# New order of TensorE's steps in the experts, the cross-attention and the feed-forward of a four-module transformer kernel

## What is computed

```python
# L0: experts. cond and ctx (77 rows) are given per batch
nx = layer_norm(x); k, v = ctx @ Wk, ctx @ Wv
weights = softmax(nx @ Wq @ k.T / 16)                    # 77 keys
combined = concat([nx, weights @ v, cond])
probs = softmax(combined @ router_W + router_b)          # 3 experts
h = silu(combined @ e_w1[e] + e_b1[e])                   # 256*3 -> 512 each
routed = sum(probs[e] * (h @ e_w2[e] + e_b2[e]))
g = sigmoid(silu(combined @ gate_w1) @ gate_w2)
x = x + g * (routed @ out_w + out_b)
# L1: self-attention, cross-attention, feed-forward, 16 heads of 16
x = x + attn(ln(x), ln(x)) + t_sa; x = x + attn(ln(x), ctx, mask) + t_ca
x = x + gelu(ln(x) @ w1 + b1) @ w2 + t_mlp               # 256 -> 1024 -> 256
# L2: the same three with modulated norms and gates, tanh gelu
# L3: cross-attention with adaptive norms of both sides
```

## Time and profile before

| what | us |
| --- | --- |
| median of three runs | 3690.1 (3686.6 to 3706.2) |
| profiled execution | 3701.9 |
| its span, first to last instruction | 3700.1 |
| TensorE busy | 3394.4 |
| ScalarE busy | 2302.2 |
| VectorE busy | 2223.0 |
| GpSimd busy | 871.0 |

### The profile page before, as it was taken

How to read it: one execution, slowest core, us unless ns; L and a number is a source line. 1 busy time by engine, 2 the same in 40 slices (tenths; PEclk the granted TensorE clock), 3 DMA queues, 4 the chain that set the end, 5 groups by cost and what they waited for, 6 DMA issues and landing times.

```text
span 3700.1 us, 60840 instructions
## 1 busy us (share of the span) xinstructions
PE 3394.4 (92%) x22433; PEld 2000.9 (54%) x22433; DVE 2223.0 (60%) x3645; ACT 2302.2 (62%) x3983; POOL 871.0 (24%) x578
## 2 busy tenths in 40 slices
PE   8999998999899898998998889989998899899988
PEld 6767766444643564446444744455446444564465
DVE  2323324794397556953794559746955488549654
ACT  2333332787578555875786457865875578658764
POOL 0322322103400431015103420052024200340061
PEclk8989989999999999999999999999999999999999
DMA  5011012110100001110010010100100101000100
GB/s 184 1 36 35 2 36 63 32 16 26 39 8 14 13 13 57 14 30 31 13 16 15 12 57 11 22 26 26 14 19 13 58 7 26 24 28 11 22 13 13
DMA packets 226988, 101.25 MB, mean 27 GB/s; under 512 B 159951, under 2 KB 210322, under 8 KB 226582
## 3 DMA queue, kind: packets, MB, share of 16 engines
q1 hardware_dynamic: 201734, 77.21, 8.4%
q10 hardware_dynamic: 24976, 20.15, 1.8%
HBM read 79.31 MB, written 9.96 MB: 24 GB/s over the span
## 4 chain that ended last, share of the span: by engine, by line
PE 79%; DVE 12%; ACT 5%; issue 2%; POOL 1%; DMA 0%; SPq 0%; ACTq 0%; DVEq 0%; POOLq 0%
PE ps L736 76%; DVE mxh L1791 4%; PE ps L1184 2%; DVE ctxk L1740 2%; DVE ow L1823 1%; ACT probs L1470 1%; DVE tok L1526 1%; PE ps L1045 1%; DVE small L1510 1%; DVE x L1757 1%; DVE mx L1788 1%; POOL small L1847 1%; ACT qs L1439 1%; ACT whole L1424 1%; ACT hT L1256 1%
## 5 line engine op out<-in xcount | busy, mean ns | idle before, releaser
L1470 ACT ACTIVATE probs<-ps 128x512 f32<-128x512 f32 (+1 forms) x2176 | 1220.4, 639 | 222.3 <-PE ps L736 169.7
L1791 DVE TENSOR_REDUCE mxh<-ps 128x2 f32<-128x1024 f32 x1024 | 1232.1, 1220 | 101.2 <-PE ps L736 96.3
L736 PE MATMUL ps<-probs,v 128*32 128x256 f32 (+2 forms) x8064 | 732.8, 435 | 9.7 <-ACT probs L1470 6.3
L736 PE MATMUL ps<-ks,qs 64*128 64x512 f32 x2048 | 502.4, 491 | 51.5 <-DVE mxh L1791 23.3
L736 PEld LDWEIGHTS ps<-ks,qs 64*128 64x128 f32 x2048 | 193.0, 183 | 445.8 <-issue 347.7
L736 PE MATMUL ps<-qs,ks 64*128 64x512 f32 x2048 | 425.5, 413 | 4.0 <-DVE mxh L1791 3.0
L1911 POOL TENSOR_TENSOR hT<-hT,tok 128x512 f32<-128x512 f32 (+1 forms) x32 | 40.9, 1279 | 1221.1 <-DMA tok<-weights_of_outputs 1221.1
L736 PEld LDWEIGHTS ps<-probs,v 128*32 128x32 f32 (+1 forms) x8064 | 160.0, 107 | 302.7 <-ACT probs L1470 249.1
L736 PEld LDWEIGHTS ps<-qs,ks 64*128 64x128 f32 x2048 | 244.0, 184 | 127.6 <-ACT probs L1470 105.9
L1788 DVE TENSOR_REDUCE mx<-ps 128x4 f32<-128x312 f32 x384 | 166.3, 477 | 150.9 <-PE ps L736 147.4
L736 PE MATMUL ps<-hT,slot 128*128 128x512 f32 x448 | 235.5, 659 | 21.2 <-issue 8.5
(11 more groups left out here) (226 smaller groups left out, 5893.9 us busy)
## 6 DMA issues: line engine op xcount, KB each, us to landing
qs<-mx SPq DMA_DIRECT2D x896, 0.5 KB, 2.0
slot<-in_L_w SPq DMA_DIRECT2D x8, 1024.0 KB, 10.0
slot<-in_L_fc_w SPq DMA_DIRECT2D x8, 1024.0 KB, 5.2
hT<-ow SPq DMA_DIRECT2D x48, 128.0 KB, 2.7
tok<-weights_of_outputs SPq DMA_DIRECT2D x192, 32.0 KB, 1.9
xin<-in_x ACTq DMA_DIRECT2D x5, 1024.0 KB, 5.9
x_after_block<-x ACTq DMA_DIRECT2D x20, 256.0 KB, 2.3
xin<-x_after_block SPq DMA_DIRECT2D x5, 1024.0 KB, 5.5
```

Source lines behind the costliest of these rows:

```text
L736: return pe.matmul(out, lhsT, rhs, start=start, stop=stop)
L1470: ins = act.activation(dst, src, ACT.Exp, scale=SCALE)
L1791: dve.tensor_reduce(mxh[:, z, t, j // 2, j % 2, :], ps[:, a:a + 2, :], AX.X, ALU.max, negate=True).then_inc(dve_done, M.add(dve_done, name))
```

## The change

In the experts, for all but the first pass, the first two key products go ahead of the scores and wait only for what the pass before had done by its gate products. In the first pass they also go ahead of the scores, behind the same waits. VectorE copies them first. Only two first-layer groups stand ahead of the turn of the weights, the other two behind it. `affine_split` writes `hTh` and `whole` of one column block before those of the other. In the cross-attentions `OT` goes behind `PV` and the second pair of `S`. In front of a feed-forward two `up` of half 0 stand ahead of the turn of half 1, and GpSimd's `rsqrt` of half 1 stands at `N` 1, behind its split of half 0, instead of behind `o` 3.

```diff
@@ pass_schedule, cross_attention @@
             if u < len(units):
                 put(tag, ("S",) + units[u] + (0,), *last[4 * u:4 * u + 2])
-            if u > lag:
-                put(tag, ("OT",) + units[u - lag - 1][:2])
             if u >= lag:
                 put(tag, ("PV",) + units[u - lag], ("O",) + units[u - lag][:2])
             if u < len(units):
                 put(tag, ("S",) + units[u] + (2,), *last[4 * u + 2:4 * u + 4])
+            if u > lag:
+                put(tag, ("OT",) + units[u - lag - 1][:2])
...
-        put(follow, ("T", 0), ("N", 1), ("T", 1), *[("up", 0, m) for m in range(FM)])
+        put(follow, ("T", 0), ("N", 1), ("up", 0, 0), ("up", 0, 1), ("T", 1), *[("up", 0, m) for m in range(2, FM)])
@@ tensor, experts @@
+                def last(sem, *steps):
+                    return M.upto("experts", it - 1, sem, steps)
+
+                def evidence_of_keys(e):
+
                     b, act_was, dve_was = take(("L0", "u", e), dve=("L0", "u", e))
-                    pe.wait_ge(act_done, upto(act_done, *act_was))
-                    pe.wait_ge(dve_done, upto(dve_done, *dve_was))
+                    if e < 2 and it:
+                        pe.wait_ge(act_done, last(act_done, ("next", "kv"), *act_was))
+                        pe.wait_ge(dve_done, last(dve_done, *dve_was))
+                    else:
+                        pe.wait_ge(act_done, upto(act_done, *act_was))
+                        pe.wait_ge(dve_done, upto(dve_done, *dve_was))
...
+                if not it:
+                    owner.clear()
+                    pe.wait_ge(act_done, upto(act_done))
+                    pe.wait_ge(dve_done, upto(dve_done))
+                held = [evidence_of_keys(e) for e in range(2)]
+                if it:
+                    owner.clear()
+                    owner.update({b: ("dve", ("L0", "u", e)) for e, b in enumerate(held)})
+                    pe.wait_ge(act_done, upto(act_done))
+                    pe.wait_ge(dve_done, upto(dve_done))
+                for n in range(NH):
...
+                for e in range(2, E + 1):
+                    evidence_of_keys(e)
...
-                early = [hidden(0, m) for m in range(4)]
+                early = [hidden(0, m) for m in range(2)]
...
                     ins.then_inc(mm_done, M.add(mm_done, ("L0", "wT", n)))
+
+                early += [hidden(0, m) for m in range(2, 4)]
@@ scalar, affine_split @@
-                for c in range(KC):
+                    act.wait_ge(mm_done, upto(mm_done, (tag, "T", n, KC - 1)))
                     act.activation(whole[:, KC * n + c, :], ps[:, M.where((tag, "T", n, c)), :], ACT.Identity, bias=shift(c),
@@ vector, experts @@
+                for e in range(2):
+                    keys_copied(e)
                 for n in range(NH):
...
-                for e in range(E + 1):
...
+                for e in range(2, E + 1):
+                    keys_copied(e)
@@ gpsimd, blocks @@
-                    elif kind == "o" and step[1] % 2 and tag in NEXT_LN:
+                    elif kind == "o" and step[1] % 2 and tag in NEXT_LN and not (step[1] == 3 and NEXT_LN[tag] in ("ln2", "ln6")):
                         rsqrt(upto, NEXT_LN[tag], step[1] // 2)
+                    elif kind == "N" and step[1] and KIND[tag] == "mlp":
+                        rsqrt(upto, ln, 1)
```

More of the change, by code:

```diff
@@ L886, in _ @@
                     ins.then_inc(mm_done, M.add(mm_done, ("L0", "u", e)))
+                    return b
+                if not it:
[9 more added lines that the diff above has]
+                for n in range(NH):
+                    b, act_was, dve_was = take(("L0", "s", n), act=("L0", "e", n, TPH - 1))
+                    for i in range(TPH):
+                        t = TPH * n + i
+                        for k in range(KC):
+                            ins = mm(ps[:, b, i * SW:(i + 1) * SW], whole[:, KC * n + k, i * P:(i + 1) * P], a0[:, k, :], k == 0, k == KC - 1)
+                    ins.then_inc(mm_done, M.add(mm_done, ("L0", "s", n)))
+                for e in range(2, E + 1):
+                    evidence_of_keys(e)
                 def hidden(n, m):
```

20 lines of the change are left out of this document (5 added, 15 removed).

## The result

The changed kernel takes 3628.6 us (3626.3 to 3632.0, four runs) where the kernel before takes 3693.6; the ratio is 0.9825, with a 95% interval of 0.9801 to 0.9849. A second set of runs gave 0.9834 (0.9812 to 0.9856). The time lies in the predicted range, 15.6 us above the predicted 3613. The profiled execution took 3626.3 us against 3701.9 before, so 75.6 us went between the two profiles, where the sum of the prediction had 77. By the medians of the two sets it is less, 65.0 and 60.3 us: the profiled run of the kernel before was one of its slower ones.

The account below looks back on a forecast made before the run. TensorE, busy 92% of the span, bounds the kernel; only its idle or half-clock time can go. 26.7 + 2.8 + 2.7 + 10.2 + 24 + 9.6 + 0.6 = 77 us off 3701.9 gives 3625, median 3613; range 3590 to 3635.

Parts of the forecast that it names:

- Keys early: Experts, passes 1 to 3: two key products ahead of the scores gain 8.9 us a pass, 26.7 us in three.
- The first pass: Experts, pass 0: with key products first the clock comes back sooner, a gain of 2.8 us.
- Router: Experts: splitting first-layer groups around the weights' turn removes TensorE's 0.67 us wait four times, 2.7 us.
- The clock term: Experts, at the router: fewer falls to half clock, 10.2 us as the middle of 0 and 20.4.
- Cross-attention: Twelve loops: OT behind PV and the second scores gains 2.0 us each, 24 us; bounds 0.5 and 2.9 per loop.
- Feed-forward: Eight fronts: first up-product 0.9 us earlier plus 0.3 for the clock, 9.6 us; bounds 0 and 3 each.
- From profile to median: Whole kernel: the profiled execution lies 11.8 us above the median of three runs, so 3625 us becomes 3613.
- (a): Experts: the clock falls at the router in all passes and during the scores; 3632 us, chance 0.15.
- (b): Cross-attention loops and feed-forward fronts give nothing, as VectorE's chain sets the end there; 3647 us, chance 0.12.
- (c): Experts: early key products are held until `whole` is there, so only their place changes; 3640 us, chance 0.09.
- (d): Cross-attention loops: new clock falls, 5.1 us each, make it slower; two per loop give 3735 us, chance 0.04.
- What would show it: Trace signs: experts pass 125 to 135 us, clock 1.00 at scores, OT's wait about 11 us, 150 to 220 at half clock.

## Why the prediction was right, and where it was off

*Keys early.* Right in mechanism and size. The stretch from the first key product to the first layer takes 16.44 us, forecast 16.8; the scores 3.69, forecast 3.9. A pass with no fall at the router is 14.6 us shorter than before, forecast 8.9 + 0.7 + 5.1 = 14.7. Half of the 8.9 is the clock, as the run with the extra product shows by itself. The first pass is 8.2 us shorter, where 2.8 + 0.7 + 5.1 = 8.6 was forecast, but this is no test: with the same code of the experts it took 160.3 to 166.7 us in the other profiles, and 165.9 in two profiles with the key products behind the scores and no fall in it. (Nor was it one of four passes of 143.4 us, as the prediction has it: it took 171.4 before.)

*Router.* The wait on `wT` is gone, worth 0.5 us a pass instead of 0.67. The clock term was taken as the middle, 10.2 us; in the profile after it was 17 (4 x 5.1, less 3.4 for the one fall of 6.8 us). That makes 42.4 us of forecast into 48.7 in the experts. In the second profile three falls took 10.2 of the 20.4 back, which is the forecast. A middle was the right choice, but for a reason that I didn't have: the term isn't a fixed number of the code. Nor is what it is taken from: I counted four falls in the kernel before, and two profiles with the experts' order of before have two and three.

*Cross-attention.* 22.5 us for 24 forecast, and 21 to 23 alone. OT's wait went to 6.6 us, below the 11 that I expected, and 5.6 us came up as the wait for the tokens, 0.47 us a loop, which the allowance of 0.2 was too small for.

*Feed-forward.* The term that failed: 9.6 us forecast, 2.9 in the profiles, and alone 4 us by medians, which can't be told from nothing. The first up-product does start 0.8 us ahead of the old turn, and the turn of the second half waits for nothing. But I priced the start and not the idle time. Before, one transpose of the second half already ran in the middle of the gap, a row that I passed over beside the earlier trace rows:

```profile
1282.90 0.30 PE L1045 MATMUL ps<-ident,tok 128*128 128x128 f32 x1 [3.25 <-DVE tok L1526]
```

So TensorE idled 3.25 + 0.88 = 4.13 us there, and now idles 3.64. Over the eight fronts that is 33.0 us before and 29.1 after, a gain of 3.9 us and not 8 x 0.9; and in L2 the wait for the context, which the sum took as nothing, rose from 5.7 to 9.7 us. In the feed-forwards as a whole TensorE idled 43.0 us before and 43.6 after. What they gained is busy time, with 44.4 us at half clock instead of 47.8, which is 0.2 us a front where I had added 0.3 for an earlier return of the clock. Last, I took two up-products as 2.7 us at full clock; at half clock they take 4.4 (887.54 to 891.96). Alone, L1 gained 1.0 us a front and L2 lost 0.2; in the profile after it is 0.6 and 0.2 gained.

*From profile to median.* The largest error. I took the profiled execution to lie 11.8 us above the median, from three runs. The 25 runs of before in the next set have a median of 3698.3, so it lay 3.6 us above, and the profiled run of after lay 2.3 us below its own median. 11.8 + 2.3 = 14.1 of the 15.6 us come from this. The sum itself was off by 1.4 us between the two profiles, with +6.3 at the experts, -1.5 at cross-attention and -6.7 at the feed-forward against each other, and that it came so close is in part luck: by medians the change is worth 65.0 and 60.3 us, 12 to 17 under the sum, and the second profile of the changed kernel lies 68.7 us under that of before.

*The rivals.* (a) The clock did follow at the scores, and at the router in three passes of one profile and one of the other. On transposes, which by the Trainium skill (TensorE: Matmul & The Clock Gate, Part 4: PE-mode transpose) don't count as busy in the same way, no run here gives a proof: the turn of the weights stood right ahead of the router in the run with the keys early alone, and the clock fell in two passes of four. (b) It was right about the fronts of the feed-forwards and wrong about the loops. (c) is out by the row at 324.07. (d) didn't come with this change. Its mechanism is real, though, and dearer than I priced it: 5.1 us a fall was taken from the experts, but in a cross-attention loop the clock doesn't come back, and one fall at its start cost 15.7 us. Four such loops cost 63 us, about what the whole change had won. The range of 3590 to 3635 wasn't the sum of the bounds that I had written down: with 0 and 20.4 at the router, 0.5 and 2.9 a loop, 0 and 3 a front it is 3578 to 3651.

*What would show it.* An experts pass of 128.8 to 131.8 us (125 to 135), clock 1.00 at the scores, 187 us at half clock (150 to 220), first up-product ahead of the second turn: as said. OT's wait fell further, to 6.6 us where 11 was said.

## What to carry to other kernels

Idle time in front of narrow products costs more than its length: fill it with any wide product that is ready, and look at the clock, not only at the wait, when you price it. Where the clock falls at a place in some profiles of the same code and not in others, price the place by how often it falls, and take totals from many runs before you correct a profile by a few microseconds. Price an earlier start by the idle time that it removes, with every instruction that already runs in the gap, and not by the start. Before an edit that lets a stage start earlier is given its worth, follow the stage to its end on VectorE and GpSimd: the wait may stand ten microseconds further on, and moving that step can make a loop start with a gap that it never recovers from.

## What the runs showed of the hardware

*A VectorE step can be held by GpSimd for many instructions.* The same `tensor_scalar` on 77x256 values takes 0.41 us alone, 3.68 beside one GpSimd instruction of 3.60, and 14.65 beside nine in a row that end 0.15 us ahead of it. I had read the 3.26 instead of 1.38 us in the earlier trace rows as a matter of two microseconds. The Trainium skill (SBUF — State Buffer, Who interferes with whom) has it that a VectorE instruction in a two-port mode, which `tensor_scalar` can enter, and a GpSimd instruction exclude each other, and that the one issued first keeps the shared ports for its whole instruction. The trace agrees for one instruction (no row shows the mode) and goes further, since VectorE didn't get in between the nine. Each of them starts ahead of the end of the one before (1250.77 against 1246.19 + 4.63); in the variant with the step ahead of the loop GpSimd's next instruction starts 0.07 us behind the end of the first (1193.25 against 1189.58 + 3.60), and VectorE did get in, ending at 1193.32. Whether the pause is what let it in isn't shown.

*The clock can stay down under full work.* In the cross-attention's loop, where the products stream 512 columns over 64 or 77 rows, those with `probs` against 32 columns of values, TensorE is busy for 29.93 of 30 us at 0.50, and the clock isn't raised; the same loop, entered at 1.00 with 8% of idle time, keeps 1.00. It stayed down, for 27 to 31 us, in all eight such loops of the two kernels with the step ahead of the loop. Why it isn't raised no run shows.

*The fall at the router depends on more than the code:* one and three of four passes in two profiles of the same kernel; never over 6.8 us long with the keys early, 6.8 or 10.2 us with the order of before.
